# Second LayerNorm moved from inside the first FFN product to the group boundaries, and the q/k projections moved three steps later in the attention

## The reference

```python
x = x + attn(layernorm(x), W_qkv, W_out)   # 16 heads of 64, causal softmax
x = x + ffn(layernorm(x), w1, b1, w2, b2)  # 1024 -> 4096, relu, 4096 -> 1024

# attn: out has the shape (b, n, q, h) and is reshaped to (b, 1024, S);
# W_out is summed over heads and head rows: einsum('bds,nhd->bsd', out, W_out)
# ffn: relu(einsum('bsd,dw->bsw', x, w1) + b1), then einsum('bsw,wd->bsd', h, w2) + b2
```

## Time and profile before

| | us |
|---|---|
| median of the timed runs (1354.15 and 1355.72) | 1354.94 |
| the profiled execution, its own time | 1337.32 |
| its span, on the slowest core (core 5) | 1335.8 |
| spans of the eight cores | 1320.6 to 1335.8 |
| mean granted TensorE clock of the cores | 0.881 to 0.892 |

### The profile page before, as it was taken

One profiled execution on the slowest core, in us unless ns is written; L12 is line 12 of the kernel. 1 busy time (PEld: TensorE's weight loads), 2 busy tenths in 40 slices (PEclk: granted clock), 3 DMA queues, 4 the chain that ended last, 5 costly groups with the idle time before them and its releaser, 6 DMA issues.

```text
span 1335.8 us, 12735 instructions; the slowest of 8 cores (1320.6 to 1335.8 us)
## 1 busy us (share of the span) xinstructions
PE 988.9 (74%) x4656; PEld 389.3 (29%) x4656; DVE 471.4 (35%) x638; ACT 412.3 (31%) x443; POOL 79.9 (6%) x107
## 2 busy tenths in 40 slices
PE   1279789585858586776756466795789956999997
PEld 0134322131312132222211232342334322444443
DVE  0541242636354544445353742004230322203401
ACT  0124166574757566675766110000000000000000
POOL 2100200000000000000000001020001100020010
PEclk9989878696969798887967698898899978999999
DMA  8920701010000002000200199995348923598476
GB/s 188 180 12 1 71 9 17 1 16 0 9 9 0 1 0 32 0 1 1 32 0 1 35 192 173 185 153 144 95 126 126 184 88 106 126 154 193 126 114 139
DMA packets 102652, 101.57 MB, mean 76 GB/s; under 512 B 40128, under 2 KB 81088, under 8 KB 102592
## 3 DMA queue, kind: packets, MB, share of 16 engines
q0 software_dynamic: 60288, 50.41, 27.9%
q10 hardware_dynamic: 33280, 33.56, 8.1%
q1 hardware_dynamic: 9024, 16.80, 4.2%
HBM read 134.37 MB, written 16.78 MB: 113 GB/s over the span
## 4 chain that ended last, share of the span: by engine, by line
PE 61%; DVE 15%; DMA 14%; issue 3%; DVEq 3%; ACT 3%; POOL 0%; ACTq 0%; POOLq 0%
PE arena L792 17%; PE arena L742 11%; PE arena L524 11%; PE arena L381 9%; PE arena L469 5%; DMA wstage<-w1b 5%; DVE tmp_sb L633 4%; PE arena L303 4%; DVE oscr_sb L540 3%; DVE x_sb L644 3%; DMA wstage<-w 3%; DMA wstage<-wqkv 3%; DVEq L54 2%; DMA wstage<-wout 2%; DMA w1b<-wstage 2%
## 5 line engine op out<-in xcount | busy, mean ns | idle before, releaser
L497 ACT ACTIVATE p_sb<-arena,cst_sb 128x1024 bf16<-128x1024 f32 (+1 forms) x320 | 291.1, 987 | 101.0 <-PE arena L469 61.9
L524 PE MATMUL arena<-p_sb,vaug_h 128*128 128x512 bf16 (+3 forms) x640 | 194.8, 390 | 142.1 <-DVE oscr_sb L540 94.2
L742 PE MATMUL arena<-lnf_sb,wstage 128*128 128x512 bf16 x1024 | 246.6, 403 | 58.4 <-DMA wstage<-w1b 40.9
L792 PE MATMUL arena<-w2stage,h_sb 128*128 128x512 bf16 x1024 | 221.7, 379 | 4.4 <-DVE h_sb L757 4.4
L757 DVE TENSOR_SCALAR h_sb<-arena,b1c_sb 128x512 bf16<-128x512 f32 x128 | 95.3, 749 | 205.0 <-PE arena L742 205.0
L742 PEld LDWEIGHTS arena<-lnf_sb,wstage 128*128 128x128 bf16 x1024 | 103.3, 103 | 196.0 <-issue 94.5
L792 PEld LDWEIGHTS arena<-w2stage,h_sb 128*128 128x128 bf16 x1024 | 99.9, 98 | 126.1 <-issue 6.2
L381 PE MATMUL arena<-lnf_sb,wstage 128*128 128x512 bf16 x512 | 125.8, 403 | 8.6 <-DMA wstage<-wqkv 8.6
L469 PE MATMUL arena<-qpair,kpair 64*128 64x512 bf16 (+3 forms) x640 | 126.5, 391 | 4.9 <-DVE kpair L404 4.9
L524 PEld LDWEIGHTS arena<-p_sb,vaug_h 128*128 128x128 bf16 x640 | 42.7, 100 | 205.6 <-issue 204.3
L819 DVE TENSOR_TENSOR y_sb<-arena,x_sb 128x512 f32<-128x512 f32 x32 | 19.5, 681 | 224.1 <-PE arena L806 224.1
(11 more groups left out here) (37 smaller groups left out, 439.8 us busy)
## 6 DMA issues: line engine op xcount, KB each, us to landing
w2stage<-w POOLq DMA_DIRECT2D x64, 512.0 KB, 6.4
wstage<-w1b ACTq DMA_DIRECT2D x24, 1024.0 KB, 5.3
x_sb<-x SPq DMA_DIRECT2D x4, 2048.0 KB, 14.4
wstage<-w POOLq DMA_DIRECT2D x8, 1024.0 KB, 10.5
w1b<-wstage ACTq DMA_DIRECT2D x8, 1024.0 KB, 7.0
y<-y_sb SPq DMA_DIRECT2D x16, 512.0 KB, 7.0
wstage<-wqkv POOLq DMA_DIRECT2D x24, 256.0 KB, 11.7
wstage<-wout POOLq DMA_DIRECT2D x4, 512.0 KB, 18.5
```

What stands on the lines that cost most here:

```text
L497: e.activation(AP(p_sb, (si_ % 3) * 1024, [[3 * 1024, 128], [512, 2], [1, w_]]), AP(arena, b_ + off_, [[AR, 128], [512, 2], [1, w_]]), AF. ...
L524: e.matmul(AP(arena, (4 + hx) * 512 + off_, [[AR, 128], [1, w_]]), vaug_h[:, hx, j_ * 128:(j_ + 1) * 128], AP(p_sb, (si_ % 3) * 1024 + hx ...
L742: e.matmul(bankap(fb_, TF), AP(wstage, s_ * 1024 + dc_ * 512 + wp_ * 128, [[8 * 1024, 128], [1, 128]]), lnf_sb[:, dc_, lp_:lp_ + TF], star ...
L792: (lambda s_, ww_, c2_, dh_, t_: lambda e: e.matmul(bankap(t_, 512), h1_sb[:, ww_, 128 * c2_:128 * (c2_ + 1)], w2stage[:, s_, 512 * dh_:51 ...
```

## The change

Three edits.

1. `ck_slots` becomes {11, 20, 29, 38}: each block of q/k projections comes three steps later.
2. The LayerNorm of group g+1 leaves FFN1 of group g. Its DVE part and the square root are emitted behind FFN2's matmuls of group g (ahead of the sums L819). Its transposes and copies are emitted at the head of group g+1, ahead of that group's first load of `w1b` in ACT's queue.
3. These transposes use banks 0 to 3 instead of 6 and 7; the first two wait for the sums of banks 0 to 3 (`ffn2_evac4`). `lnf_sb` has one half in use instead of two.

```diff
-            ck_slots = {8, 17, 26, 35} if next_chunks else set()
+            ck_slots = {11, 20, 29, 38} if next_chunks else set()
...
-                for t in range(4):
-                    extra_tp = [("ex", ex_attn_done)] if t <= 1 else []
-                    ln_transpose(lnf_sb, lpar + t * 128, t,
-                                 ln2_apps[g % 2][t], extra_tp=extra_tp)
+            for t in range(4):
+                c = g * 4 + t
+                extra_tp = ([("ex", ex_attn_done)] if (g == 0 and t <= 1)
+                            else ([ffn2_evac4] if (g > 0 and t <= 1) else []))
+                ln_transpose(lnf_sb, t * 128, t, ln2_apps[g % 2][t],
+                             extra_tp=extra_tp)
             vv_ln2 = lnf_state["ready"]
...
             for ww in range(NWW):
-                if g + 1 < NG:
-                    if ww == 2:
-                        vst = ln_stats((g + 1) * 4 + 0, ((g + 1) % 2) * 4)
-                        vst = ln_stats((g + 1) * 4 + 1, ((g + 1) % 2) * 4 + 1)
-                    elif ww == 4:
-                        vst = ln_stats((g + 1) * 4 + 2, ((g + 1) % 2) * 4 + 2)
-                        vst = ln_stats((g + 1) * 4 + 3, ((g + 1) % 2) * 4 + 3)
-                        ln2_rstd[(g + 1) % 2] = ln_rstd(((g + 1) % 2) * 4,
-                                                        4, vst)
-                    elif ww in (6, 10, 14, 18):
-                        t = (ww - 6) // 4
-                        app = ln_apply_only((g + 1) * 4 + t,
-                                            ((g + 1) % 2) * 4 + t, t,
-                                            ln2_rstd[(g + 1) % 2])
-                        ln_transpose(lnf_sb, ((g + 1) % 2) * 512 + t * 128,
-                                     t, app,
-                                     extra_tp=(ob67 if t == 0 else ()),
-                                     bank67=True)
...
+            if g + 1 < NG:
+                vst = 0
+                for t in range(4):
+                    vst = ln_stats((g + 1) * 4 + t, ((g + 1) % 2) * 4 + t)
+                ln2_rstd[(g + 1) % 2] = ln_rstd(((g + 1) % 2) * 4, 4, vst)
+                ln2_apps[(g + 1) % 2] = [
+                    ln_apply_only((g + 1) * 4 + t, ((g + 1) % 2) * 4 + t,
+                                  t, ln2_rstd[(g + 1) % 2],
+)
+                    for t in range(4)]
             out_bank_free = []
```

More of the change, by code:

```diff
@@ L237, in ln_apply_only @@
                 waits=[("vv", vv_rstd)], inc="vv")
-        ln67_state = {"free": None}
         def ln_transpose(dst_sb, dst_tok0, parity, vv_app, extra_tp=(),
-                         buf=None, np_=4, free_tbl=None, bank67=False):
+                         buf=None, np_=4, free_tbl=None):
             buf = lntm_sb if buf is None else buf
@@ L245, in ln_transpose @@
             pb = parity % np_
-            base = 6 * 512 if bank67 else (2 * (pb % 2)) * 512
-            bfree = ln67_state["free"] if bank67 else ln_bank_free[pb % 2]
             tp_last = None
             for dc in range(DC):
-                w0 = (([("vv", vv_app)] + ([bfree] if bfree else []) +
-                       [("dwb", 32)] + list(extra_tp)) if dc == 0 else [])
-                tp_last = add("tensor", (lambda p_, dc_, b_, ba_: lambda e:
+                w0 = ([("vv", vv_app), ln_bank_free[pb % 2],
+                       ("dwb", 32)] + list(extra_tp)) if dc == 0 else []
+                tp_last = add("tensor", (lambda p_, dc_, b_: lambda e:
                                          e.matmul(
-                    AP(arena, ba_ + dc_ * 128,
+                    AP(arena, (2 * (p_ % 2)) * 512 + dc_ * 128,
                        [[AR, 128], [1, 128]]),
@@ L257, in ln_transpose @@
                     identb[:, :], start=True, stop=True,
-                    skip_group_check=True))(pb, dc, buf, base),
+                    skip_group_check=True))(pb, dc, buf),
                     waits=w0, inc="tp" if dc == DC - 1 else None)
             free_tbl[pb] = ("tp", tp_last)
-            ex_ev = add("scalar", (lambda t0, d_, ba_: lambda e: e.activation(
+            ex_ev = add("scalar", (lambda t0, p_, d_: lambda e: e.activation(
                 d_[:, :, t0:t0 + 128],
-                AP(arena, ba_, [[AR, 128], [128, 8], [1, 128]]),
+                AP(arena, (2 * (p_ % 2)) * 512,
+                   [[AR, 128], [128, 8], [1, 128]]),
                 AF.Identity))(
-                dst_tok0, dst_sb, base),
+                dst_tok0, pb, dst_sb),
                 waits=[("tp", tp_last)], inc="ex")
[L267 to L270, removed]
+            ln_bank_free[pb % 2] = ("ex", ex_ev)
             lnf_state["ready"] = ("ex", ex_ev)
@@ L672, in build_program @@
         for g in range(NG):
-            lpar = (g % 2) * 512
             if g == 0:
@@ L684, in build_program @@
                     for t in range(4)]
-                for t in range(4):
-                    extra_tp = [("ex", ex_attn_done)] if t <= 1 else []
-                    ln_transpose(lnf_sb, lpar + t * 128, t,
-                                 ln2_apps[g % 2][t], extra_tp=extra_tp)
+            for t in range(4):
[4 more added lines that the diff above has]
+                             extra_tp=extra_tp)
             vv_ln2 = lnf_state["ready"]
-            ob67 = ([out_bank_free[6], out_bank_free[7]]
-                    if out_bank_free else [("ex", ex_attn_done)])
             for ww in range(NWW):
-                if g + 1 < NG:
-                    if ww == 2:
-                        vst = ln_stats((g + 1) * 4 + 0, ((g + 1) % 2) * 4)
-                        vst = ln_stats((g + 1) * 4 + 1, ((g + 1) % 2) * 4 + 1)
-                    elif ww == 4:
-                        vst = ln_stats((g + 1) * 4 + 2, ((g + 1) % 2) * 4 + 2)
-                        vst = ln_stats((g + 1) * 4 + 3, ((g + 1) % 2) * 4 + 3)
-                        ln2_rstd[(g + 1) % 2] = ln_rstd(((g + 1) % 2) * 4,
-                                                        4, vst)
-                    elif ww in (6, 10, 14, 18):
-                        t = (ww - 6) // 4
-                        app = ln_apply_only((g + 1) * 4 + t,
-                                            ((g + 1) % 2) * 4 + t, t,
-                                            ln2_rstd[(g + 1) % 2])
-                        ln_transpose(lnf_sb, ((g + 1) % 2) * 512 + t * 128,
-                                     t, app,
-                                     extra_tp=(ob67 if t == 0 else ()),
-                                     bank67=True)
                 if ww % 4 == 0:
@@ L740, in build_program @@
                     mm_f1 = add("tensor",
-                                (lambda s_, dc_, fb_, wp_, lp_: lambda e:
-                                 e.matmul(
+                                (lambda s_, dc_, fb_, wp_: lambda e: e.matmul(
                                     bankap(fb_, TF),
@@ L746, in build_program @@
                                        [[8 * 1024, 128], [1, 128]]),
-                                    lnf_sb[:, dc_, lp_:lp_ + TF],
+                                    lnf_sb[:, dc_, 0:TF],
                                     start=(dc_ == 0), stop=(dc_ == DC - 1),
-                                    skip_group_check=True))(
-                                    s, dcc, fb, wpar, lpar),
+                                    skip_group_check=True))(s, dcc, fb, wpar),
                                 waits=w0,
@@ L764, in build_program @@
             vv_h1 = C["vv"]
-            ln67_g = ln67_state["free"] if g + 1 < NG else None
             for ww in range(NWW):
@@ L786, in build_program @@
                             w0 += [("vv", vv_h1)] + out_bank_free
-                    elif t == 6 and ww == 0 and ln67_g is not None:
-                        w0 = [ln67_g]
                     elif t == 7:
```

## The result

| | before | changed |
|---|---|---|
| median of all timed runs, us | 1353.47 | 1323.91 |
| ratio to before | | 0.9806, 95% interval 0.9769 to 0.9844 |
| span of the profiled execution, us | 1335.8 | 1320.4 |
| spans of the eight cores, us | 1320.6 to 1335.8 | 1304.0 to 1320.4 |
| mean granted clock of the cores | 0.881 to 0.892 | 0.865 to 0.877 |

What follows compares the result with a forecast made beforehand. It took the kernel as bound by TensorE with gaps, mainly FFN1's late weight loads. Boundaries 32.4, group 0 6.0 and blocks 0 sum to 38.4 us won; 1354.9 - 38.4 = 1316.5, say 1316 us, range 1299 to 1337.

Steps and rivals of the forecast that it cites:

- FFN1 freed of the LayerNorm: FFN1 of groups 1 to 3 without LayerNorm takes 56.6 us, plus 1.9 us for PE's cold start.
- DVE's part under FFN2: LayerNorm statistics and normalisations on DVE, some 12 us, run under FFN2's 57 us and cost nothing.
- Rival F: In FFN2, POOL and DVE exclude each other, delaying loads up to 3.5 us each: 10.5 us, 1327 us; chance 0.05.
- The boundary: New gap ahead of FFN1 in groups 1, 2 and 3: 1.2 + 4.2 + 8.0 + 0.1 = 13.5 us.
- the landing: At the boundary, quad 0's load lands in 8.0 us, bounded by 5.3 and about 12.
- Group 0: Its FFN1, bound by transfers, gains 6.0 us as quad 3's load leaves 8 us earlier; bounds nothing to 9.3.
- The blocks: Attention's projection blocks three steps later: net -0.1 us a pair, taken as 0; bounds 18 us lost, 10 won.
- rival C: In attention, the third block delays the epilogue's exps instead of hiding: 18 us less won, 1334 us; chance 0.13.
- The sign that the prediction set: Pairs of heads in the attention differing from before by over 1 us each would show the forecast wrong.
- the cover by the reciprocal: Right behind an epilogue, ACT's reciprocal covers the third block: idleness falls from 3.59 to about 1.1, 2.5 us won.
- the 17.6 us: Whole kernel: the timed median's distance above the profiled execution of before, carried over unchanged to the forecast.
- The cause of the slow FFN1: FFN1 of groups 1 and 2 loses 35 and 38 us because weight loads queue behind LayerNorm work on ACT.

Runs made afterwards that it cites:

- e9: e2 with quad 1's w1b load in groups 1 to 3 held until FFN1's first matmuls are done; quad 0's load landed in mean 9.6 us, against 11.2.
- e2: The changed kernel with the projection blocks back at slots 8, 17, 26, 35, only the LayerNorm moved: 0.9736 of before, 35 us faster.
- e1: The kernel before with only the projection blocks moved to slots 11, 20, 29, 38: 1.0136 of before, 18 us slower.
- e3: e2 with only the third projection block three steps later (slot 29): 0.9664 of before, pair of heads 70.6 us.
- e10: e2 with only the first projection block three steps later (slot 11): no ratio, pair of heads 74.6 us on cores 0 to 3.
- e6: The kernel before with the w1b loads of groups 1 to 3 issued from POOL's queue instead of ACT's: 0.9735 of before, 36 us faster.
- e4: e2 with only the second projection block three steps later (slot 20): 0.9916 of before, pair of heads 75.0 us.

## Why the prediction was right, and where it was not

- **FFN1 freed of the LayerNorm, 56.6 us plus 1.9 for the cold start: right.** 58.6 us on core 0, 58.9 in the mean.
- **DVE's part under FFN2 costs nothing: right.** FFN2 57.0 to 57.2 us on all cores. Rival F's mechanism is at most there in small: while the four normalisations of group 0's boundary ran (867.90 to 871.44), one POOL issue took 0.975 us, where the longest of this line before was 0.745. No matmul waited, and the price was 0.27 us, not 3.5. The Trainium skill, "SBUF — State Buffer", "Who interferes with whom", says that with DVE in a two-port mode the one of DVE and GpSimd that comes second is blocked for the whole instruction. The traces agree in part only: on each of the eight cores one issue is longer (0.945 to 0.977 us), and three others that overlap the same instructions in groups 1 and 2 take 0.70 to 0.71 as without them.
- **The boundary, 13.5 us: the term of the landing was too small.** 1.2 + 4.0 + 10.7, 15.9 us on core 0, and 16.5 in the mean. The prediction took 8.0 from the case where one load left 7 us behind the first store. Here two leave 5 us behind it. It named the successor but gave it no price; e9 puts it at 1.1 to 1.7 us. 3 x 2.7 = 8 us of the sum. The sentence that quads 0 and 1 were loaded during FFN2 before holds for quad 0 alone: the earlier trace rows have quad 1's load at 920.99, inside FFN1.
- **Group 0, 6.0 us: 8.4 measured.** The load of quad 3 left 16.4 us after the first matmul of FFN1 (793.60 on core 0) and not 22.6, 6 us earlier where 8 was forecast.
- **FFN together: 38.4 predicted, 32.8 in the stretches, 35 in the timed runs of e2.**
- **The blocks, 0: wrong; 18 us lost (e1).** This is rival C in size, not in mechanism, and I had given it 0.13. The sign that the prediction set, pairs that differ by over 1 us, was there: 2.8. What failed is that every block was costed at 3.5 us and alone. "Its idleness should fall to about 1.1" for the third block: it fell to 2.94, because the block ran at a granted clock of 0.69 and took 5.19 us. At the same place with the clock at 1.00 it is 1.25 (e3), so the cover by the reciprocal was read rightly. "Its idleness should rise to the fourth's", 2.62, for the second: it rose to 4.06, the cover lost as forecast and 1.4 us of lower clock on top. The 5.35 us of the earlier trace rows had shown what a cold stretch does to 16 matmuls, but nothing in the rows told where the clock would fall, and e10 shows that the first block's place alone makes the second slow.
- **The sum came near by luck for the larger part.** The direction was the FFN's, and right. But by the profiled executions the prediction is 1298.9 and the measurement 1322.0, 23 us more: 17 by the blocks, 9 by the boundaries, less 3 by group 0. The 1316 was made by carrying over the 17.6 us between two timed runs of before (1354.15 and 1355.72) and its profiled execution. In the changed kernel this distance is 1.9 us, and other timed runs of before come down to 1341.0. So 15.7 us of the miss were hidden by a term that had nothing to do with the change.
- **The cause of the slow FFN1** was put down to ACT's queue. e6 shows that this is 19 us of 36 a group. The change removes both halves, so the forecast didn't suffer.

## What to carry to other kernels

A DMA issued from a computing engine's queue inherits every wait in front of it. Look at what stands ahead of each load in its queue, and hoist the load or move it to another queue, before the work itself is moved. Filler work on PE belongs where the engine it starves is busy with something else, here just behind the reciprocal on ACT, and its cost has to be taken at the clock that PE has at that place. Two edits in one change should be timed apart: here one was worth 35 us and the other cost 18. And a distance between timed and profiled executions that rests on two runs is no constant to carry over.

## What the runs showed of the hardware that I had not expected

The granted clock in the attention changes with how the gaps and the dense work lie, and small moves shift whole pairs: with the same work a pair took 70.6 us at a mean clock of 0.84 (e3), 71.7 at 0.83 (e2), and 74.6 at 0.80 (e1). The mean clock is not the whole of it: e4 has 75.0 us at 0.82, where ACT's cover is lost too. Within the changed kernel single pairs took 72.4 to 75.2 us. The third block of 16 matmuls, at one and the same place, took 3.61 us at a granted clock of 1.00 (e3) and 5.19 at 0.69 (changed).

With four 512 KB stores that left up to 5 us earlier, and a load of w2, in flight on other queues, a 1 MB load landed in 9.6 us instead of 5.3, and with one more load behind it in 10.7 to 11.2. The Trainium skill, "DMA: Bandwidth & Descriptors", "Queues, rings and completion order", says that each DMA engine goes round between the queues that have work for it. The 9.6 us beside other queues agree with that; the successor's 1.1 to 1.7 us are within one queue, of which that sentence says nothing.
